# A GNN kernel on one core: what tells the other engines that TensorE's transposes and sums are done, and where the sums stand between its products

## The reference, cut to what matters

```python
def gnn_layer(feat, efeat, W_msg, b_msg, W_attn, b_attn, src, dst):   # 6250 nodes, 200000 edges, 16 features
    w_m = (efeat @ W_msg + b_msg).reshape(E, 16, 16)
    w_a = (efeat @ W_attn + b_attn).reshape(E, 16, 16)
    h_src = feat[src][:, :, None]
    e1, e2 = w_m * h_src, w_a * h_src
    ex = exp(e2 - segment_max(e2, dst)[dst])
    attn = ex / segment_sum(ex, dst)[dst]
    return segment_sum(e1 * attn, dst).sum(axis=1)
mean = segment_sum(edge_attr, dst) / max(counts, 1)
x = layernorm(x + gnn_layer(x, edge_attr, ...))
out = layernorm(x + mean)
```

## Time and profile before

| | us |
|---|---|
| median of 3 runs | 3010.83 |
| lowest and highest run | 2994.75, 3017.14 |
| span of the profiled execution, first to last instruction | 2950.2 |
| PE, DVE, ACT, POOL busy | 2137.9, 1862.0, 1256.9, 1687.5 |
| mean granted TensorE clock | 0.861 of full |

### The profile page before, as it was taken

How to read it: one execution, slowest core, us unless ns; L and a number is a source line. 1 busy time by engine, 2 the same in 40 slices (tenths; PEclk the granted TensorE clock), 3 DMA queues, 4 the chain that set the end, 5 groups by cost and what they waited for, 6 DMA issues and landing times. The chain is left out here.

```text
span 2950.2 us, 21765 instructions
## 1 busy us (share of the span) xinstructions
PE 2137.9 (72%) x6682; PEld 952.6 (32%) x6682; DVE 1862.0 (63%) x2907; ACT 1256.9 (43%) x1228; POOL 1687.5 (57%) x1845
## 2 busy tenths in 40 slices
PE   2347676676877777877787658877787767887777
PEld 1213233232333333333333223333333323333333
DVE  6246465566666666666676547766667656786776
ACT  3223443434444443454454325444444444554444
POOL 6556355665655565555565465655656565655633
PEclk8658888897988888989888889988989888988988
DMA  6000000000000000000000000000000001001000
GB/s 229 16 10 11 8 12 10 10 10 9 10 9 9 14 10 9 10 14 10 10 13 9 9 10 13 10 12 9 10 12 9 12 9 28 12 8 16 8 2 3
DMA packets 60073, 47.60 MB, mean 16 GB/s; under 512 B 28366, under 2 KB 55439, under 8 KB 59436
## 3 DMA queue, kind: packets, MB, share of 16 engines
q0 software_dynamic: 57632, 29.73, 8.0%
q1 hardware_dynamic: 2316, 16.38, 1.5%
HBM read 44.00 MB, written 1.90 MB: 16 GB/s over the span
## 5 line engine op out<-in xcount | busy, mean ns | idle before, releaser
L652 POOL DMA_INDIRECT AR<-in_xt,AR x1607 | 1538.8, 958 | 974.1 <-DVE AR L1472 491.3
L1128 PE MATMUL PX<-AR,CS 128*128 128x512 f32 x3246 | 1663.7, 642 | 37.8 <-issue 23.9
L1472 DVE CUSTOM_DVE_ANT_1 AR<-PW,AR 128x1024 f32<-128x1024 f32 x815 | 979.6, 1221 | 896.8 <-remote 651.2
L1108 PE MATMUL PW<-WS,LT 100*128 100x512 bf16 x1630 | 549.1, 423 | 683.9 <-DVE AR L1472 511.8
L1128 PEld LDWEIGHTS PX<-AR,CS 128*128 128x128 f32 x3246 | 664.9, 206 | 652.1 <-issue 532.4
L888 ACT ACTIVATE LT<-PTB 100x1024 bf16<-100x1024 bf16 (+1 forms) x221 | 211.2, 956 | 1005.7 <-remote 601.0
L1485 DVE TENSOR_TENSOR AR<-AR,PX 128x1024 f32<-128x1024 f32 (+1 forms) x442 | 501.0, 1134 | 121.3 <-ACT PX L944 76.0
L1108 PEld LDWEIGHTS PW<-WS,LT 100*128 100x128 bf16 x1630 | 141.5, 103 | 1113.7 <-DVE AR L1472 543.2
L946 ACT ACTIVATE AR<-AR 128x2048 f32<-128x2048 f32 (+1 forms) x221 | 412.9, 1869 | 7.2
L950 ACT ACTIVATE PX<-AR 128x1024 f32<-128x1024 f32 (+1 forms) x221 | 212.4, 961 | 412.3 <-DVE AR L1485 294.8
L944 ACT ACTIVATE PX<-AR 128x1024 f32<-128x1024 f32 (+1 forms) x221 | 231.0, 1045 | 39.4 <-DVE AR L1485 30.1
(11 more groups left out here) (192 smaller groups left out, 517.7 us busy)
## 6 DMA issues: line engine op xcount, KB each, us to landing
AR<-in_xt,AR POOLq DMA_INDIRECT x1607
AR<-in_eat SPq DMA_DIRECT2D x3, 3128.0 KB
AR<-in_eat SPq DMA_DIRECT2D x1, 3120.0 KB
y_d<-AR SPq DMA_DIRECT2D x1, 784.0 KB
AR<-y_d SPq DMA_DIRECT2D x1, 784.0 KB
AR<-in_es,E0I POOLq DMA_INDIRECT x48
y_d<-AR POOLq DMA_INDIRECT x36
CS<-in_cst SPq DMA_DIRECT2D x1, 442.0 KB, 5.3
```

What stands on the lines that cost most here:

```text
L652: g.indirect_dma_start(feat(h, j - j0, j - j0 + 1), None, xt, bass.IndirectOffsetOnAxis(ap=node, axis=0)).then_inc(hg_sem(h), 16)
L1108: i = pe.matmul(PAIRS[s % 2][:, j, :], LT[:, g % 3, lo:lo + 128], WS[:, :], start=True, stop=True)
L1128: i = pe.matmul(PDR, IDN, x, start=(a == 0 and j == 0), stop=(g == LAST[k] and j == n - 1))
L1472: v.tensor_tensor_reduce(em(g, j, j + 2).rearrange("p (x c) -> p x c", c=32), w, hb, 1.0, LOW, ALU.mult, ALU.max, accum_out=MXC[:, k % 2, ...
```

## The change

Two things change together.

1. A transpose group signals `p_T` only for groups 0 and 1, and the sums of a group signal `p_g` only for the last six groups (215 to 220, `BY_SELF`), behind which no product follows. For all others the waiting engine waits on `p_W` for the next product behind them on PE. As PE works through its list in order, that product's signal says that the transposes or sums ahead of it are done too. `PAST_T[g]` and `PAST_G[g]` are the counts of products issued up to there. This concerns ACT's `evac`, `first`, `second` and `sums`, and DVE's `low` and `mult`. DVE drops the second wait where the product that it needs anyhow is already past the old sums, which holds for all but 21 groups.
2. The sums of a group stand between the products of the step: with four products in a step behind the first, second and third (2, 3 and 3 slots) and none behind the fourth; with three products behind the first and second (4 and 4), none behind the third; with fewer all behind the first (`SPAN`). The transposes stand where they stood, behind the second turn's sums.

PE's signals in this path are then 2 + 815 + 6. Its matrix instructions are the same 6682.

```diff
+SPAN = {4: [(0, 2), (2, 5), (5, 8)], 3: [(0, 4), (4, 8)], 2: [(0, 8)], 1: [(0, 8)], 0: [(0, 8)]}
+def TURNS(i):
+    a = len(AHEAD(i))
+    return [(AHEAD(i)[x] if x < a else None, SPAN[a][x] if x < len(SPAN[a]) else (8, 8)) for x in range(max(a, 2))]
+PAST_T, PAST_G, w = {0: 0, 1: 0}, {}, 2
+for i in range(NST):
+    p, old = STEPS[i][0] if i < len(STEPS) else None, STEPS[i - 1][1] if 1 <= i <= len(STEPS) else None
+    for x, (ahead, (lo, hi)) in enumerate(TURNS(i)):
+        w += ahead is not None
+        if x == 1 and p is not None and p + 2 < NGR:
+            PAST_T[p + 2] = w
+        if old is not None and lo < GRP[old][2] <= hi:
+            PAST_G[old] = w
+BY_SELF = [g for g in range(NGR) if PAST_G[g] == len(PAIR)]
...
                 def evac(g):
-                    a.wait_ge(S["p_T"], g + 1)
-                    if g >= 3:
-                        a.wait_ge(S["p_W"], FROM[g - 2])
+                    if g < 2:
+                        a.wait_ge(S["p_T"], g + 1)
+                    else:
+                        a.wait_ge(S["p_W"], PAST_T[g] + 1)
...
                 def sums(k):
-                    a.wait_ge(S["p_g"], LAST[k] + 1)
+                    if LAST[k] in BY_SELF:
+                        a.wait_ge(S["p_g"], BY_SELF.index(LAST[k]) + 1)
+                    else:
+                        a.wait_ge(S["p_W"], PAST_G[LAST[k]] + 1)
...
                     for j in range(n):
                         i = pe.transpose(PTB[0:K, 128 * j:128 * j + 128], part(k, 0, K)[:, j0 + j, :], IDB[:, :])
-                    i.then_inc(S["p_T"], 1)
+                    if g < 2:
+                        i.then_inc(S["p_T"], 1)
...
-                        if j == n - 1:
+                        if j == n - 1 and g in BY_SELF:
                             i.then_inc(S["p_g"], 1)
...
-                    for x in range(4):
-                        if x < len(ahead):
-                            W(*ahead[x])
+                    for x, (ahead, (lo, hi)) in enumerate(TURNS(i)):
+                        if ahead is not None:
+                            W(*ahead)
                         if old is not None:
-                            gsum(old, 2 * x, 2 * x + 2)
+                            gsum(old, lo, hi)
                         if x == 1 and p is not None and p + 2 < NGR:
                             T(p + 2)
...
                         v.wait_ge(S["v_hm"], HMS[g])
-                        if OLD[g] is not None:
-                            v.wait_ge(S["p_g"], OLD[g] + 1)
+                        if OLD[g] is not None and PAST_G[OLD[g]] > s:
+                            v.wait_ge(S["p_W"], PAST_G[OLD[g]] + 1)
```

More of the change, by code:

```diff
@@ L149, in KEPT, with AHEAD @@
     return (n + 1) // 2
+def AHEAD(i):
+    p = STEPS[i][0] if i < len(STEPS) else None
+    nx = STEPS[i + 1][0] if i + 1 < len(STEPS) else None
+    rest = [(p, x) for x in range(2, GRP[p][2] // 2)] if p is not None else []
+    return rest + ([(nx, 0), (nx, 1)] if nx is not None else [])
+SPAN = {4: [(0, 2), (2, 5), (5, 8)], 3: [(0, 4), (4, 8)], 2: [(0, 8)], 1: [(0, 8)], 0: [(0, 8)]}
[12 more added lines that the diff above has]
+BY_SELF = [g for g in range(NGR) if PAST_G[g] == len(PAIR)]
+assert w == len(PAIR) and max(PAST_T.values()) < w
+assert all(OLD[g] is None or PAST_G[OLD[g]] <= FROM[g] + 1 for g in range(NGR))
 def gnn_kernel(nc, xt, dst, src, ea, eat, es, wc, cst, cst2, out):
@@ L910, in first @@
                     if k >= 2:
-                        a.wait_ge(S["p_T"], LAST[k - 2] + 1)
+                        a.wait_ge(S["p_W"], PAST_T[LAST[k - 2]] + 1)
                     a.activation(part(k, 99, 100)[:, 1:d, :], VLD[:, 1:d].unsqueeze(2), ACT.Relu, bias=1.0, scale=-1.0).then_inc(S["a_p"], 1)
@@ L1138, in regular @@
                     p, c = STEPS[i] if i < len(STEPS) else (None, None)
-                    nx = STEPS[i + 1][0] if i + 1 < len(STEPS) else None
                     old = STEPS[i - 1][1] if 1 <= i <= len(STEPS) else None
-                    ahead = [(p, x) for x in range(2, GRP[p][2] // 2)] if p is not None else []
-                    ahead += [(nx, 0), (nx, 1)] if nx is not None else []
-                    for x in range(4):
-                        if x < len(ahead):
-                            W(*ahead[x])
+                    for x, (ahead, (lo, hi)) in enumerate(TURNS(i)):
+                        if ahead is not None:
+                            W(*ahead)
                         if old is not None:
-                            gsum(old, 2 * x, 2 * x + 2)
+                            gsum(old, lo, hi)
                         if x == 1 and p is not None and p + 2 < NGR:
@@ L1445, in low @@
                     if k >= 2:
-                        v.wait_ge(S["p_T"], LAST[k - 2] + 1)
+                        v.wait_ge(S["p_W"], PAST_T[LAST[k - 2]] + 1)
                     x = RM[:, 0:DEG[k], :]
```

## The result

| | before | after |
|---|---|---|
| median of the runs, us | 3012.53 (4 runs) | 3069.76 (4 runs) |
| lowest and highest | 2994.75, 3017.14 | 3045.10, 3079.46 |
| span of the profiled execution | 2950.2 | 3077.0 |
| mean granted clock | 0.861 | 0.846 |

The ratio is 1.0206, with a 95% interval from 1.0146 to 1.0267: **the change makes the kernel 2% slower**. 2830 us was forecast, with a range of 2670 to 2950, so the time lies outside it and on the other side.

What follows compares the result with a forecast made beforehand. PE's signals, late while POOL issues gathers, were taken to bound the kernel. Fewer signals save 191 us, ACT's later copy costs 10: 3010.8 - 181 = 2830 us, range 2670 to 2950.

Steps and rivals of the forecast that it cites:

- What bounds the kernel: PE's signals to DVE and ACT come up to 9 us late while POOL issues gathers one behind the other.
- In the late part one signal costs 6.5 / 1.54 = 4.2 us: PE's signals past a gather run's first 10 us: 4.2 us each, so a product there falls from 6.5 to 4.25 us.
- The whole term of 154 to 228 us: Saving from 434 fewer PE signals, through shorter pauses of POOL's gathers; the middle, 191 us, was taken.
- signals leave in bunches: Rival: POOL's issuing time counts, not the number of PE's signals; 0 to 65 us saved, 2946 to 3011 us; chance 0.12.
- a signal costs next to nothing: Rival: DVE's remote waits are something else, such as a DMA; 17 us saved, 2994 us; chance 0.03.
- The skill's price: Trainium skill's rule of some 26 ns for each matmul signal on PE; an estimated 11 us for 434 signals.
- I cost both at nothing: PE's sums between products: next step's first product and the later last product cost nothing; uncovered, 172 us over 143 steps.
- The 21 groups that wait for the last product: DVE's first multiplication waits for the step's last product, 0.6 us later each; 13 us at most, put at nothing.
- The later wait of ACT's copy: ACT's copy out of PTB waits for the next product, delaying exponentials and DVE's `gm`; 10 us put, 53 bound.
- The rival on the slower side: ACT held by products: waits reach `gm` through ACT's exponentials, 233 us on top, 3090 us with the lower gain; chance 0.06.

Runs made afterwards that it cites:

- The drains: Kernel before with POOL waiting after every 4, 5, 6, 8 or 16 gathers of tiles 2 to 47 until they landed; ratios to before from 0.8835 to 0.9905.
- the kernels with few gathers: Kernels with one gather for each group instead of 6 or 8, output not the reference's; before's version took 2154.5 us, the changed kernel's 2313.2 us.
- drain_6: Kernel before with POOL waiting after every 6 gathers of tiles 2 to 47 until they have landed; 2650.0 us, 0.8835 of before.
- drain_5: Kernel before with POOL waiting after every 5 gathers of tiles 2 to 47 until they have landed; 2705.4 us, 0.9214 of before.
- drain_4: Kernel before with POOL waiting after every 4 gathers of tiles 2 to 47 until they have landed; 2808.4 us, 0.9456 of before.
- more_signals: Kernel before with each slot of sums that gave no signal signaling a semaphore nobody waits for, 2660 signals instead of 1257; 2979.3 us, 0.9981 of before.
- all_signals: Changed kernel with every transpose group and every group's sums signaling again, 1257 signals instead of 823; 3037.1 us, 1.0183 of before.
- few_pack: Kernel before with only the sums' new places, old signals and waits kept, and one gather for each group; 2270.2 us against 2154.5.
- few_after: Changed kernel with one gather for each group, other slots' features left out; 2313.2 us, 0.7720 of the full kernel before.
- few_before: Kernel before with one gather for each group instead of 6 or 8, other features left out; 2154.5 us, 0.7189 of the full kernel before.
- few_signals: Changed kernel's signals and waits with the sums' old places, and one gather for each group; 2191.5 us against 2154.5.
- signals_only: Changed kernel with the sums back in their old places, 20 groups keeping their own signal; 2995.6 us, 1.0060 of before.
- evac_wait: Kernel before in which only ACT's copy out of PTB waits for the product behind the transposes; 2997.9 us, 1.0013 of before.
- drain_8: Kernel before with POOL waiting after every 8 gathers of tiles 2 to 47 until they have landed; 2787.7 us, 0.9356 of before.
- drain_16: Kernel before with POOL waiting after every 16 gathers of tiles 2 to 47 until they have landed; 2944.4 us, 0.9905 of before.
- the second drain_6: Kernel before with POOL's wait after every 6 gathers, run once more beside the changed kernel with the same wait; 2654.7 us, 0.8898 of before.

## Why the prediction was wrong

**What bounds the kernel: right, and borne out.** PE's signals are late because of POOL's gathers. The drains and the kernels with few gathers show it from both sides: with shorter runs of gathers there are fewer remote waits and, down to 6 gathers, less time; with next to no runs there are next to no remote waits, and 837 us less. In the kernel before, the cut of the earlier trace rows holds: all 51 of DVE's remote waits that end while POOL still issues end more than 10 us into its run. It is no fixed threshold. In drain_6, 55 of the 70 remote waits (154 of 249 us) stand at runs of gathers shorter than 10 us (the six of drain_5 and the five of drain_4 all at longer ones), so a pause of 1.7 us doesn't always clear the lateness. Whether the unbroken run counts or the rate of gathers over a dozen or more, no experiment separates: each drain lowers both.

**"In the late part one signal costs 6.5 / 1.54 = 4.2 us": this step failed.** I divided the time of a product by the number of signals and took the quotient for a price, because signals arrive in order and so each seemed to hold up the next. Arriving in order doesn't mean that each takes its turn. more_signals shows 1403 more of them to be worth -0.2% (-0.6 to +0.2%), and all_signals with 434 more is no slower than the change. Both add signals that nobody waits for; the price was to hold for every signal in line. The whole term of 154 to 228 us was made of that price, and the two runs leave no room for it. The rival "signals leave in bunches" was nearer, with what counts being how long POOL goes on and not how many stand in line, and I gave it 0.12. Its own range ended at no saving, which is what more_signals shows for a pure change of their number. The rival "a signal costs next to nothing", at 0.03, had the price right and the source of the waits wrong.

**The skill's price.** By the rule of the Trainium skill (TensorE: Matmul & The Clock Gate, "The cost: per-tile semaphore tail"), 434 signals are worth an estimated 11 us. For those 434 the runs allow it: all_signals, which gives them again, can't be told from the change. At the same rule's price of 26 ns the 1403 more signals of more_signals would be an estimated 37 us, and that run shows 6 us more at the most, so not even that much is paid for each. I set the small price aside because late signals take microseconds; the lateness is real, but it is no cost of a signal.

**"I cost both at nothing": this step failed too, and gives the larger part of the loss.** I wrote that the last product comes two slots later and looked at who needs the multiplication behind it, on PE. I did not look at who waits for the product itself: DVE's second multiplication of the group, for which no cover was worked out. few_pack measures it: 116 us where signals are prompt, two thirds of the 172 us that I had named as the price without cover, and at another place of the step. Beside late signals 1.2% is left, some 36 us.

**The 21 groups that wait for the last product: right.** I put 13 us at most and nothing in the sum. In few_after one of them waits 2.38 us:

```profile
1323.32 0.60 PE L1144 MATMUL PW<-WS,LT 100*128 100x512 bf16 x2
...
1324.05 1.23 DVE L1505 CUSTOM_DVE_ANT_1 AR<-PW,AR 128x1024 f32<-128x1024 f32 x1 [2.38 <-PE PW L1144]
```

The same multiplication of few_before waits as long, there for the sums themselves:

```profile
1259.76 1.88 PE L1128 MATMUL PX<-AR,CS 128*128 128x512 f32 x4
1261.77 1.23 DVE L1472 CUSTOM_DVE_ANT_1 AR<-PW,AR 128x1024 f32<-128x1024 f32 x1 [2.39 <-PE PX L1128]
```

Before these 21 multiplications DVE stands idle for 47.3 us in few_before and 47.0 in few_after.

**The later wait of ACT's copy: right mechanism, right bound, size too small.** I named that ACT's copy holds up the exponential for which `gm` waits, bounded it by 53 us and put 10. few_signals measures 37 us, with 46 us more of just that wait. On the full kernel signals_only costs 0.6%, 18 us; evac_wait, the later wait of the copy alone, shows 0.1% (-0.3 to +0.6%), so on the full kernel it is not shown that the copy makes the 0.6%.

**The rival on the slower side** had this mechanism but a size that needed all steps; the kernel became slower by another one, the spacing, which I had priced and dismissed. I gave a slower kernel 0.06 in all, though a cost of 172 us stood in my own text beside a gain that rested on one division.

**What remains open.** Why gathers delay PE's signals, and why the delay doesn't grow with their number, no run shows; nor whether it is POOL's issuing or the transfers that follow from it, since each drain pauses both. The ends of matmuls are modelled in the profile, so the traces can't tell a late signal from a matmul that started on time and ended late. The late part's 8.1 us a product after the change, against 6.5, is not settled either: products that come in pairs lose a whole late spell where spaced ones lose part of it, but that is only argued, and of the two profiled executions one is quicker than all of its kernel's runs and the other among the longest.

## What to carry to other kernels

A queue that delivers late is not yet a queue that charges by the piece: before dividing a delay by a count, double the count in one experiment. Where an engine waits for the products of another one by one, keep them evenly spaced; work moved ahead of one product is paid by whoever waits for that product, so ask this for each, not for the step as a whole. When signals come late while an engine issues small indirect transfers one behind the other, try letting it pause on its own, and try several lengths: here a wait after every 6 gathers gave 11% or more with no other change, after every 16 only 1%.

## What the runs showed of the hardware that I had not expected

PE's signals, prompt within 0.04 us, come up to 9 us late while GpSimd issues gathers of 128 rows back to back, and in the earlier trace rows are all there within 3.2 us of its last one. That is not the rule: of the kernel before's 123 remote waits of DVE 51 end while GpSimd still issues, and 14 of the other 72 end later than 3.2 us after its last DMA, up to 7.0. In this kernel none ends within the first 10 us of a run of gathers, but with short pauses between the runs some do. A pause, of 1.7 us on average, after every 5 gathers leaves 32 us of DVE's remote waits instead of 651, after every 6 249 (314 in the second trace), after every 8 458, after every 16 657. The waits of drain_6:

```profile
POOL AR L652 <- DMA AR<-in_xt,AR: 346.8, 205, 2.8
...
DVE AR L1474 <- remote: 248.9, 70, 24.3
```

The times vary less where signals are prompt: the runs of drain_4, drain_5 and the kernels with few gathers each lie within 0.5%, those of drain_8, drain_16 and the second drain_6 within 1.2 to 1.5%. That the lateness causes this is not shown; drain_6 did both, 0.5% in one set and 1.2% in the other.
